# Second mixture of a two-layer MetaFormer kernel: expert weights gathered by GpSimd's indirect DMAs instead of loaded by SyncE's DMAs with a register offset

## The chip, the cores and the metric

The program runs on one core of one Trainium2 chip. The metric is the device time of one execution in microseconds. The median of the kernel before is 3442.44 us over 2 runs (3441.41 and 3443.48).

## The reference

Sixteen images of 64 channels and 56 x 56 pixels pass through two layers. Each layer has a convolution block and a mixture-of-experts block, with norms over the channels ahead of each. Only the second mixture is touched. Its routing is one choice per image: two experts of eight, with two weights.

```python
# x: 16 images, each 3136 tokens of 64 channels; E = 8 experts, hidden size 128
logits = mean(x, axis=1) @ Wr + br
routing_weights = softmax(logits)                    # per image
expected_loads = routing_weights.sum(axis=0) * (N / B)
scale = where(expected_loads > capacity, capacity / expected_loads, 1.0)
routing_weights = softmax(routing_weights * scale)
top_w, top_i = top_k(routing_weights, 2); top_w = softmax(top_w)
h = gelu(x @ W1[e] + b1[e])                          # exact gelu, per expert
y = h @ W2[e] + b2[e]
out = layer_norm(sum over the 2 chosen of top_w * y + x, gamma, beta)
```

## The kernel before

The kernel is written engine by engine, with semaphores by hand, in seven blocks that follow each other with a barrier between them. The image data `X` stays in SBUF for the whole program as 56 tiles of 128 partitions x 448 pixels: 8 pairs of images (the 64 channels of one image on partitions 0 to 63, those of its partner on 64 to 127), 7 tiles to a pair. Blocks 1 to 5 do the first layer and the second convolution. Block 6 (from line 1072) computes the routing on 8 partitions. It also splits the first weight matrices of all 8 experts into a coarse and a fine half and writes them to the DRAM scratch `W1D` as [8 experts, 128 rows, 2, 128]. At its end it writes the chosen expert numbers (`IDX`, 8 pairs x 4) and their weights (`WSEL`) to DRAM.

Block 7 (from line 1202) is the one that changes. It works pair by pair, p = 0 to 7, and each pair uses 4 experts q (two for each image). Two buffers b = p % 2 hold a pair's expert data:

- `w1s`, in the trace `w1sel`: 128 x 256 floats for each q.
- `w2r`, in the trace `w2raw`: 128 x 64 floats for each q.
- `b1s`, in the trace `b1sel`: one float per partition for each q.
- `b2r`, in the trace `b2raw`: two columns, each half of the partitions from another expert.

All loads of one buffer count on one semaphore, `w_in[b]`.

- **SyncE (SP)** issues every DMA of the block: first the expert numbers, the routing weights, gamma and beta, then the tokens of pair 0 (`S[:, k]`, in the trace `tokens<-scr_split`, and `u[:, k]`, `tokens_plus_y<-scr_xn`). `load_weights(p, b)` loads the expert data: for each q a `value_load` of the expert number into registers, then four DMAs whose DRAM address is that register. In the loop, `load_weights(p + 1, 1 - b)` stands at the head of pair p, ahead of the token loads and the stores of that pair.
- **TensorE (PE)** waits for `w_in[b]` at the head of a pair. Then for each tile k it computes `up` (L1318, L1319: hidden layer of expert q, coarse and fine half, into two PSUM buffers) and, one tile behind, `down` (L1332). Behind the 7 tiles come the norm's matmuls `centre` (L154) and `pe_var` (L183).
- **ScalarE (ACT)** applies gelu (L1372) to each hidden tile. After the 7 tiles it squares (L162) and takes reciprocal square roots (L194, L200).
- **VectorE (DVE)** starts by waiting for all seven constant loads (`consts`, 7 x 16). Per tile it adds the tokens (L1411) and finishes a tile of the pair before (L1403). After the 7 tiles it runs `weigh(p + 1, 1 - b)`, which waits for the next pair's `w_in` and scales `w2r` into `w2s` (L1390 to L1395). Then come the norm's three steps for each of the 7 tiles (L205, L208, L215).
- **GpSimd (POOL)** has no instruction in block 7.

The order on each engine is the order of the code: nothing is scheduled by a planner.

## Time and profile before

| | |
|---|---|
| median of 2 runs | 3442.44 us (3441.41 to 3443.48) |
| span of the profiled execution | 3438.1 us; a time of its own is not listed, so what lies around the span is the 3.3 to 5.4 us by which the two runs exceed it |
| TensorE busy | 2756.5 us (80% of the span) |
| ScalarE busy | 1594.6 us (46%) |
| VectorE busy | 1484.2 us (43%) |
| GpSimd busy | 491.1 us (14%), none of it in block 7 |
| block 7 | from 3044.5 us to the end at 3438.1 us: 393.6 us |
| first matmul of block 7 | 3065.8 us |

Times in the rows are microseconds from the start of the span. A busy share over the whole span mixes seven blocks with different limits, so block 7 has to be read by itself: its first 21 us, and one pair after another from there. "SPq" is SyncE's instruction queue. A DMA is shown there with the time of its issue; its landing is given separately.

### The profile page before, as it was taken

To read this page: it belongs to the slowest core of one execution; us is meant where nothing else is said; L and a number is where in the kernel's file an instruction comes from. 1 tells how busy PE (TensorE), PEld (TensorE's weight loads), DVE (VectorE), ACT (ScalarE), POOL (GpSimd) and SP (SyncE) were. 2 spreads that over 40 slices of the span, in tenths; PEclk is the share of its full clock that TensorE was granted. 3 is DMA by queue.
4 is the path that set the end of the run, shared out by engine and by line. 5 is a ranking of instruction groups with operands and counts; after the bars stand their busy time and mean duration, and the time that the engine had idled before them with its cause. 6 is when DMAs were issued, how large, how long until landed. Compare 5 with 4: busy or idle time off the path is not lost. (4 is left out here: it accounts for less than half of the span.)

```text
span 3438.1 us, 42133 instructions
## 1 busy us (share of the span) xinstructions
PE 2756.5 (80%) x12188; PEld 1552.0 (45%) x12188; DVE 1484.2 (43%) x2823; ACT 1594.6 (46%) x2305; POOL 491.1 (14%) x408
## 2 busy tenths in 40 slices
PE   8966334340999999999999999999777777538887
PEld 5622222220555555555555555555555555313333
DVE  6625223331344444444444444443455555414555
ACT  5612222220555555555555555555444444226666
POOL 3303223220000000000000000000254444300000
PEclk9987555655999999999999999999898889769999
DMA  4474222221433333333333333333011111144553
GB/s 143 122 159 105 70 78 69 69 69 60 99 81 81 81 88 87 86 85 86 82 81 81 81 81 81 81 81 81 18 72 72 72 72 72 72 131 142 155 158 103
DMA packets 164007, 308.41 MB, mean 90 GB/s; under 512 B 45698, under 2 KB 156130, under 8 KB 156642
## 3 DMA queue, kind: packets, MB, share of 16 engines
q1 hardware_dynamic: 163938, 307.58, 33.4%
q8 instruction: 32, 0.52, 0.1%
q14 instruction: 37, 0.30, 0.0%
HBM read 210.12 MB, written 97.39 MB: 89 GB/s over the span
## 5 line engine op out<-in xcount | busy, mean ns | idle before, releaser
L776 ACT ACTIVATE hidden<-hidden_psum,b 128x896 f32<-128x896 f32 x896 | 854.4, 1004 | 705.7 <-PE hidden_psum L725 705.6
L739 PE MATMUL y_psum<-hidden,w 128*64 128x448 f32 x3584 | 773.4, 553 | 1.8 <-DVE weighted L842 1.8
L724 PE MATMUL hidden_psum<-tokens,w1hi 128*128 128x448 f32 x1792 | 705.9, 394 | 72.6 <-DMA ident<-in_ident 69.8
L842 DVE SCALAR_TENSOR_TENSOR weighted<-y_psum,b,w_bc 128x448 f32<-128x448 f32 x448 | 306.3, 684 | 923.4 <-PE y_psum L739 909.8
L725 PE MATMUL hidden_psum<-tokens,w1lo 128*128 128x448 f32 x1792 | 660.4, 369 | 0.0
L154 PE MATMUL ln_xc<-X,centre 128*128 (+1 forms) x448 | 261.9, 673 | 332.7 <-DVE X L604 294.2
L724 PEld LDWEIGHTS hidden_psum<-tokens,w1hi 128*128 128x128 f32 x1792 | 336.7, 188 | 391.5 <-ACT hidden L776 294.2
L739 PEld LDWEIGHTS y_psum<-hidden,w 128*64 128x64 f32 x3584 | 217.7, 136 | 350.0 <-issue 244.0
L194 ACT ACTIVATE ln_r<-ln_var,eps 128x448 f32<-128x448 f32 x280 | 177.4, 634 | 405.9 <-PE ln_var L179 287.5
L725 PEld LDWEIGHTS hidden_psum<-tokens,w1lo 128*128 128x128 f32 x1792 | 338.0, 189 | 24.3
L205 DVE SCALAR_TENSOR_TENSOR ln_q<-ln_var,ln_rr 128x448 f32<-128x448 f32 x280 | 173.5, 620 | 318.9 <-DMA scr_split<-lo 211.2
L850 DVE TENSOR_TENSOR X<-X,weighted 128x448 f32 (+1 forms) x448 | 278.1, 621 | 2.9
L154 PEld LDWEIGHTS ln_xc<-X,centre 128*128 128x128 f32 x448 | 91.3, 224 | 398.8 <-issue 367.5
L208 DVE SCALAR_TENSOR_TENSOR ln_g<-ln_q,ln_r 128x448 f32<-128x448 f32 x280 | 233.9, 835 | 9.6
L1038 POOL MEMSET pad_lo<- 128x116 f32 (+1 forms) x4 | 0.8, 268 | 1622.9 <-POOLq L661 1622.9
L934 PE MATMUL conv_psum<-pad_hi,conv_sign 128*128 128x448 f32 x504 | 224.3, 445 | 2.4 <-POOL pad_lo L1046 2.4
L162 ACT ACTIVATE ln_sq<-ln_xc 128x448 f32<-128x448 f32 x224 | 120.4, 537 | 210.3 <-PE ln_xc L154 210.2
L934 PE MATMUL conv_psum<-pad_lo,conv_sign 128*128 128x448 f32 x504 | 204.8, 406 | 0.0
L183 PE MATMUL ln_var<-ln_sq,average 128*128 128x448 f32 x336 | 181.3, 629 | 22.8 <-DVE ln_q L205 17.2
L604 DVE TENSOR_TENSOR X<-X,shifted 128x448 f32 (+1 forms) x56 | 49.2, 883 | 279.6 <-POOL shifted L534 279.6
L200 ACT ACTIVATE ln_rr<-ln_r 128x448 f32<-128x448 f32 x280 | 161.5, 577 | 8.9
L1372 ACT ACTIVATE hidden<-hidden_psum,b1sel 128x448 f32<-128x448 f32 x224 | 130.5, 632 | 75.5 <-PE hidden_psum L1319 75.2
(128 smaller groups left out, 2665.5 us busy)
## 6 DMA issues: line engine op xcount, KB each, us to landing
w_bc<-scr_wtok SPq DMA_DIRECT2D x112, 896.0 KB, 10.9
tokens<-scr_split SPq DMA_DIRECT2D x112, 448.0 KB, 3.7
scr_split<-hi SPq DMA_DIRECT2D x112, 224.0 KB
scr_split<-lo SPq DMA_DIRECT2D x112, 224.0 KB
scr_xn<-xn SPq DMA_DIRECT2D x56, 224.0 KB
tokens_plus_y<-scr_xn SPq DMA_DIRECT2D x56, 224.0 KB, 2.6
out<-out_tile SPq DMA_DIRECT2D x56, 224.0 KB, 2.0
X<-in_x SPq DMA_DIRECT2D x6, 1792.0 KB, 7.6
```

The source lines that it names most:

```text
L154: pe.matmul(self.xc[:, b, 0:TW], CEN[:], x, start=True, stop=True).then_inc(self.centred, 1)
L183: pe.matmul(self.var[:, self.at(m, self.nv), 0:TW], AVG[:], self.sq[:, self.at(m, self.depth)], start=True, stop=True).then_inc(self.var_r ...
L194: act.activation(self.r[:, b], self.var[:, self.at(m, self.nv), 0:TW], ACT.Abs_reciprocal_sqrt, bias=EPS[:, eps_col:eps_col + 1]).then_inc ...
L205: dve.scalar_tensor_tensor(out=self.q[:, b], in0=self.var[:, self.at(m, self.nv), 0:TW], scalar=eps, in1=self.rr[:, b], op0=ALU.add, op1=A ...
L208: dve.scalar_tensor_tensor(out=self.g[:, b], in0=self.q[:, b], scalar=-3.0, in1=self.r[:, b], op0=ALU.add, op1=ALU.mult).then_inc(self.g_d ...
L724: pe.matmul(o, w1hi[:, s * P:(s + 1) * P], S[:, b, a, :], start=True, stop=False)
L725: mm = pe.matmul(o, w1lo[:, s * P:(s + 1) * P], S[:, b, a, :], start=False, stop=True)
L739: mm = pe.matmul(yp[C * a:C * a + C, e % 2, 0:TW], w2[:, e, c, :], hs[:, s % (2 * CH0), a, :], start=(c == 0), stop=(c == CH0 - 1))
L776: act.activation(hs[:, k % (2 * CH0)], hp[:, k % 2, :, 0:TW], ACT.Gelu, bias=b1[:, e, c:c + 1])\
L842: dve.scalar_tensor_tensor(out=pr[:, e % 2], in0=yp[:, e % 2, 0:TW], scalar=b2[:, e:e + 1], in1=WB[:, b, e, :], op0=ALU.add, op1=ALU.mult) ...
L850: dve.tensor_tensor(x, x, pr[:, e % 2], ALU.add).then_inc(summed, 1)
L934: mm = pe.matmul(o, cw[:, t9, :], src[:, pair, ROWS * k + dy:ROWS * k + dy + ROWS, dx:dx + WW], start=(t9 == 0 and part == 0), stop=(t9 == ...
```

## The change

GpSimd takes over the loading of the experts' data in block 7. Instead of one DMA with a register offset it issues indirect DMAs: each of the 128 partitions gets the DRAM row whose number stands in a column of the SBUF tile `rows_now`.

- SP loads the 32 expert numbers into all 128 partitions (`picked`) instead of one, and issues no weight DMA any more. The `value_load`s are gone.
- GpSimd fills `lane` with the partition number. VectorE computes from it and from `picked` the row numbers for all pairs (`expert_rows`: expert x 128 + partition for the first four columns, expert x 64 + partition within the half for the last two). These are eight small instructions, placed behind the wait for the constants.
- GpSimd's `load_weights` copies the pair's six columns to `rows_now`, waits for that copy, and issues 14 indirect DMAs: 12 for the four experts' `w1s`, `w2r`, `b1s`, and 2 of 128 rows for the two columns of `b2r`. Before there were 16 DMAs, four of them for `b2r`, on 64 partitions each. `WIN` follows (14 x 16).
- GpSimd issues the loads of pair 0 and of pair 1 in one go. From then on those of pair p + 1 wait for the last gelu of pair p - 1 (and for `w2_done`, `b2_done`), as SP's did, but with no other DMA ahead of them in the queue.

```diff
-            idr = sbuf(ctx, "idx", [1, NP * 4], I32)
+            picked = sbuf(ctx, "picked", [P, NP * 4], I32)
...
-            WIN = 16 * (4 * 3 + 4)
+            WIN = 16 * (4 * 3 + 2)
...
-                    sp.dma_start(idr[:], IDX.rearrange("(o j) s -> o (j s)", o=1)).then_inc(idx_in, 16)
+                    sp.dma_start(picked[:], IDX.rearrange("j s -> (j s)").partition_broadcast(P)).then_inc(idx_in, 16)
...
-                    def load_weights(p, b):
-                        for q in range(4):
-                            e = sp.value_load(idr[0:1, bass.ds(p * 4 + q, 1)], min_val=0, max_val=E - 1)
-                            sp.dma_start(w1s[:, b, q].bitcast(F32), W1D[bass.ds(e, 1)].rearrange("o p s f -> (o p) s f"))\
-                                .then_inc(w_in[b], 16)
-                            sp.dma_start(w2r[:, b, q], A["w2_l1"][bass.ds(e, 1)].rearrange("o f c -> (o f) c"))\
-                                .then_inc(w_in[b], 16)
-                            sp.dma_start(b1s[:, b, q:q + 1], A["b1_l1"][bass.ds(e, 1)].rearrange("o f u -> (o f) u"))\
-                                .then_inc(w_in[b], 16)
-                            a, s = divmod(q, 2)
-                            sp.dma_start(b2r[C * a:C * a + C, b, s:s + 1],
-                                         A["b2_l1"][bass.ds(e, 1)].rearrange("o c u -> (o c) u")).then_inc(w_in[b], 16)
...
-                            wait(sp, w2_done, p)
-                            wait(sp, b2_done, p)
-                            load_weights(p + 1, 1 - b)
...
                     load_split(0, 0)
-                    sp.wait_ge(idx_in, 16)
-                    load_weights(0, 0)
                     load_tokens(0, 0)
...
+                @block.gpsimd
+                def _(pool):
+                    pool.iota(lane[:], [[0, 1]], base=0, channel_multiplier=1).then_inc(laned, 1)
+                    pool.memset(passed[:], 0.0)
+                    pool.wait_ge(rows_done, 1)
+
+                    def load_weights(p, b):
+                        def gather(dst, src, row):
+                            pool.indirect_dma_start(out=dst, out_offset=None, in_=src,
+                                                    in_offset=bass.IndirectOffsetOnAxis(ap=now[:, b, row:row + 1], axis=0))\
+                                .then_inc(w_in[b], 16)
+
+                        pool.tensor_copy(now[:, b, :], rows_of[:, bass.ds(p, 1), :].rearrange("p o s -> p (o s)"))\
+                            .then_inc(rows_now, 1)
+                        pool.wait_ge(rows_now, p + 1)
+                        pool.tensor_tensor(passed[:], passed[:], passed[:], ALU.add).then_inc(rows_seen, 1)
+                        for q in range(4):
+                            gather(w1s[:, b, q].bitcast(F32).rearrange("p s f -> p (s f)"),
+                                   W1D.rearrange("e p s f -> (e p) (s f)"), q)
+                            gather(w2r[:, b, q], A["w2_l1"].rearrange("e f c -> (e f) c"), q)
+                            gather(b1s[:, b, q:q + 1], A["b1_l1"].rearrange("e f u -> (e f) u"), q)
+                        for t in range(2):
+                            gather(b2r[:, b, t:t + 1], A["b2_l1"].rearrange("e c u -> (e c) u"), 4 + t)
+
+                    def pair(p, b, last):
+                        if not last:
+                            if not isinstance(p, int) or p > 0:
+                                wait(pool, gelu_done, 4 * KT * p)
+                                wait(pool, w2_done, p)
+                                wait(pool, b2_done, p)
+                            load_weights(p + 1, 1 - b)
+
+                    load_weights(0, 0)
+                    every_pair(pool, pair)
...
+                    dve.wait_ge(laned, 1)
+                    dve.wait_ge(idx_in, 16)
+                    dve.tensor_copy(lanef[:, 0:1], lane[:]).then_inc(row_made, 1)
+                    dve.tensor_copy(pickedf[:], picked[:]).then_inc(row_made, 1)
+                    dve.wait_ge(row_made, 2)
+                    chosen = pickedf[:].rearrange("p (j s) -> p j s", s=4)
+                    dve.tensor_scalar(rowf[:, :, 0:4], chosen, float(F1), lanef[:, 0:1], ALU.mult, ALU.add)\
+                        .then_inc(row_made, 1)
+                    for a in range(2):
+                        half = slice(C * a, C * a + C)
+                        dve.tensor_scalar(lanef[half, 1:2], lanef[half, 0:1], float(-C * a), None, ALU.add)\
+                            .then_inc(row_made, 1)
+                        dve.wait_ge(row_made, 4 + 2 * a)
+                        dve.tensor_scalar(rowf[half, :, 4:6], chosen[half, :, 2 * a:2 * a + 2], float(C),
+                                          lanef[half, 1:2], ALU.mult, ALU.add).then_inc(row_made, 1)
+                    dve.wait_ge(row_made, 7)
+                    dve.tensor_copy(rows_of[:], rowf[:]).then_inc(rows_done, 1)
                     dve.tensor_scalar(hgam[:], gam[:], -0.5, None, ALU.mult).then_inc(scaled, 1)
```

SP's queue at the head of block 7, before: behind the constants comes one token load, then the expert numbers one by one, each with its four DMAs. The group of four DMAs stands there four times in all.

```order
L1253 DMA beta<-in_beta 64x1
L1269 DMA tokens4<-scr_split4 128x2x448
L1257 TENSOR_LOAD idx [waits p7_idx]
L1257 ISA x2
L1258 ISA
L1258 DMA w1sel<-scr_w1split 128x256
L1260 ISA
L1260 DMA w2raw<-in_w2_l1 128x64
L1262 ISA
L1262 DMA b1sel<-in_b1_l1 128x1
L1265 ISA
L1265 DMA b2raw<-in_b2_l1 64x1
```

The same place on SP with the change: the token loads of pair 0 follow the constants at once, and the next wait is one for `up` of pair 0.

```order
L1262 DMA beta<-in_beta 64x1
L1265 DMA tokens4<-scr_split4 128x2x448
L1269 DMA tokens_plus_y<-scr_xn4 128x448
L1265 DMA tokens4<-scr_split4 128x2x448
L1269 DMA tokens_plus_y<-scr_xn4 128x448
```

The weight loads have left this queue; 14 token loads stand in a row here.

VectorE at the head of block 7, before: one small instruction behind the wait for the constants, then `weigh(0, 0)`, which waits for the weights.

```order
L1423 TENSOR_SCALAR minus_half_gamma<-gamma 128x1 [waits p7_consts]
L1390 TENSOR_SCALAR w2sel<-w2raw,w_all 128x64 [waits p7_w0,p7_scaled]
L1390 TENSOR_SCALAR w2sel<-w2raw,w_all 128x64 x3
L1392 TENSOR_SCALAR b2tmp<-b2raw,w_half 128x1
L1395 SCALAR_TENSOR_TENSOR b2sel<-b2raw,w_half,b2tmp 128x1 [waits p7_b2a]
```

The same place on VectorE with the change: eight instructions that make the row numbers.

```order
L1451 CAST lane_f<-lane 128x1 [waits p7_idx,p7_laned,p7_consts]
L1452 CAST picked_f<-picked 128x32
L1455 TENSOR_SCALAR expert_rows_f<-picked_f,lane_f 128x8x4 [waits p7_row_made]
L1459 TENSOR_SCALAR lane_f<-lane_f 64x1
L1462 TENSOR_SCALAR expert_rows_f<-picked_f,lane_f 64x8x2 [waits p7_row_made]
L1459 TENSOR_SCALAR lane_f<-lane_f 64x1
L1462 TENSOR_SCALAR expert_rows_f<-picked_f,lane_f 64x8x2 [waits p7_row_made]
L1465 CAST expert_rows<-expert_rows_f 128x48 [waits p7_row_made]
L1466 TENSOR_SCALAR minus_half_gamma<-gamma 128x1
L1416 TENSOR_SCALAR w2sel<-w2raw,w_all 128x64 [waits p7_w0,p7_scaled]
```

All eight stand behind the wait for the constants, and GpSimd's gathers wait for the last of them.

GpSimd's queue in block 7 with the change (before it was empty): the two instructions ahead, the copy that waits for VectorE, and the first gathers.

```order
L1306 IOTA lane 128x1
L1307 MEMSET passed 1x1
L1316 COPY rows_now<-expert_rows 128x6 [waits p7_rows_done]
L1319 TENSOR_TENSOR passed<-passed 1x1 [waits p7_rows_now]
L1312 DMA w1sel<-scr_w1split,rows_now 128x256
L1312 DMA w2raw<-in_w2_l1,rows_now 128x64
L1312 DMA b1sel<-in_b1_l1,rows_now 128x1
```

These three gathers are repeated for each of the four experts, and two `b2raw` gathers follow: 14 in all. The same 16 rows from the copy on then stand once more for pair 1, without a wait for other engines; for pair 2 the copy waits for `p7_gelu`.

## Rows read from the trace of the kernel before

**Rows 1.** Page: span and busy time of each engine.

```profile
span 3438.1 us, 42133 instructions
...
PE 2756.5 (80%) x12188; PEld 1552.0 (45%) x12188; DVE 1484.2 (43%) x2823; ACT 1594.6 (46%) x2305; POOL 491.1 (14%) x408
```

**Rows 2.** Windows, busy us of each engine, granted clock, DMA share, GB/s.

```profile
core 0: us, PE busy (x) PEld busy (x) DVE busy (x) ACT busy (x) POOL busy (x), PEclk, DMA share, GB/s
...
3044.00:3065.00 21.00, 0.00 (x0) 0.00 (x0) 0.15 (x1) 0.00 (x0) 0.00 (x0) 0.50 0.22 54
3065.00:3070.00 5.00, 2.92 (x7) 2.13 (x8) 1.08 (x6) 2.44 (x3) 0.00 (x0) 0.50 0.95 308
3070.00:3075.00 5.00, 4.93 (x14) 2.19 (x13) 0.00 (x0) 2.54 (x4) 0.00 (x0) 0.55 1.05 390
3075.00:3095.00 20.00, 20.00 (x85) 9.03 (x85) 3.42 (x5) 12.30 (x22) 0.00 (x0) 1.00 0.69 215
```

**Rows 3.** Chain that ended last, 3040 to 3072 us: start, us, what.

```profile
3049.81 0.49 SPq L1257
...
3051.34 3.00 SPq L1260
...
3063.02 0.33 SPq L1262
3063.53 2.19 DMA b2raw<-in_b_l
3065.76 0.74 PE hidden_psum L1318
```

**Rows 4.** Timeline 2990 to 3075 us: start, us, engine, line.

```profile
3048.52 0.60 SPq L1253 DMA_DIRECT2D beta<-in_beta  x1
...
3058.09 0.15 DVE L1423 TENSOR_SCALAR minus_half_gamma<-gamma 128x1 f32<-128x1 f32 x1 [16.03 <-DMA beta<-in_beta]
```

**Rows 5.** Waits, 3075 to 3438 us: in total, times, longest.

```profile
DVE tokens_plus_y L1411 <- PE ln_xc_psum L1332: 167.7, 56, 9.6
ACT hidden L1372 <- PE hidden_psum L1319: 74.0, 105, 2.1
```

**Rows 6.** Timeline of VectorE, 3088 to 3120 us.

```profile
3099.05 0.68 DVE L1411 SCALAR_TENSOR_TENSOR tokens_plus_y<-ln_xc_psum,b2sel,tokens_plus_y 128x448 f32<-128x448 f32 x1 [2.67 <-PE ln_xc_psum L1332]
3099.65 0.73 DVE L1390 TENSOR_SCALAR w2sel<-w2raw,w_all 128x64 f32<-128x64 f32 x4
3100.30 0.20 DVE L1392 TENSOR_SCALAR b2tmp<-b2raw,w_half 128x1 f32<-128x1 f32 x1
3100.54 0.22 DVE L1395 SCALAR_TENSOR_TENSOR b2sel<-b2raw,w_half,b2tmp 128x1 f32<-128x1 f32 x1
```

**Rows 7.** Timeline of ScalarE, 3088 to 3120 us.

```profile
3094.31 1.16 ACT L1372 ACTIVATE hidden<-hidden_psum,b1sel 128x448 f32<-128x448 f32 x2 [0.70 <-PE hidden_psum L1319]
...
3114.47 1.28 ACT L1372 ACT_TABLE_LOAD   x1
```

**Rows 8.** DMA issues, 3040 to 3438 us: KB each, median us to landing.

```profile
tokens<-scr_split SPq DMA_DIRECT2D x56, 448.0 KB, 3.7
tokens_plus_y<-scr_xn SPq DMA_DIRECT2D x56, 224.0 KB, 2.6
...
w1sel<-scr_w1split SPq DMA_DIRECT2D x32, 128.0 KB, 2.0
...
b2raw<-in_b_l SPq DMA_DIRECT2D x32, 0.2 KB, 2.2
```

**Rows 9.** Line 208 alone (VectorE, two SBUF inputs), by window.

```profile
2500.00:2600.00 100.00, 18.18 (x21) 0.88 0.19 71
...
3100.00:3400.00 300.00, 30.61 (x49) 0.98 0.50 148
```

**Rows 10.** GpSimd's groups of instructions, whole span: busy, mean ns.

```profile
L1051 POOL TENSOR_TENSOR lo<-xn,hi 128x448 fp32r<-128x448 f32 x56 | 63.8, 1139 | 253.1 <-DVE hi L1012 253.1
...
L1491 POOL MEMSET const-float32-0.0<- 128x1 f32 x1 | 0.1, 99 | 0.2 <-issue 0.2
```

More of the change, by code:

```diff
@@ L1215, in build @@
             bet = sbuf(ctx, "beta", [P, 1])
-            idr = sbuf(ctx, "idx", [1, NP * 4], I32)
+            picked = sbuf(ctx, "picked", [P, NP * 4], I32)
+            pickedf = sbuf(ctx, "picked_f", [P, NP * 4])
+            lane = sbuf(ctx, "lane", [P, 1], I32)
+            lanef = sbuf(ctx, "lane_f", [P, 2])
+            rowf = sbuf(ctx, "expert_rows_f", [P, NP, 6])
+            rows_of = sbuf(ctx, "expert_rows", [P, NP, 6], I32)
+            now = sbuf(ctx, "rows_now", [P, 2, 6], I32)
+            passed = sbuf(ctx, "passed", [1, 1])
             S = sbuf(ctx, "tokens4", [P, KT, 2, TW], F32R)
@@ L1228, in build @@
                                               "scaled", "out"))
+            laned, row_made, rows_done, rows_now, rows_seen = (
+                sem(ctx, "p7_" + s) for s in ("laned", "row_made", "rows_done", "rows_now", "rows_seen"))
             w_in = [sem(ctx, f"p7_w{b}") for b in range(2)]
```

## Prediction

> **What bounds the kernel now.** I read the page first, then windows over block 7, the chain that ended last, the timeline around the first matmul, the waits, and the DMA issues. TensorE is busy for 80% of the span and GpSimd for 14% [rows 1], but those shares average seven blocks, and only block 7 changes. Two stretches of it count.
>
> The head. From 3044 to 3065 us no compute engine works except for 0.15 us of VectorE, TensorE's clock is granted at 0.50 (1.2 GHz), and DMA is at a share of 0.22 [rows 2]. The chain runs through SP's queue. A register load of an expert number takes 0.49 us, one w2 issue holds the queue for 3.00 us, a common issue takes 0.33 us and the next follows 0.51 us after it (3063.02 to 3063.53). The last of 16 weight DMAs starts at 3063.53 and lands 2.19 us later, and the first matmul starts at 3065.76 [rows 3]. VectorE has been held longer than the queue needs for the first loads: its wait for the constants ends with the landing of beta at 3058.09, 9.6 us after the issue at 3048.52 [rows 4]. Before, that was harmless, since VectorE had nothing to give to anyone until the weights came.
>
> The pairs. From 3075 to 3438 us the waits are those between the compute engines: VectorE for `down` (167.7 us), ScalarE for `up` (74.0 us) [rows 5], and no DMA is among them. The expert data of a pair are wanted first by `weigh` on VectorE, at 3099.65 us for pair 1, just behind the last token add [rows 6], and it did not wait there. So SP's weight loads cost something at the head and nothing later.
>
> **The change part by part.**
>
> *SP.* It loses 16 DMAs and four register loads per pair. In the pairs this yields nothing, since nobody waits for SP's transfers. At the head it yields only that the tokens of pair 0 start earlier: seven times 448 + 224 KB [rows 8], 4.7 MB. At the 308 to 390 GB/s seen from 3065 to 3075 [rows 2] that takes 12 to 15 us. Begun behind the constants at 3057 or so, they are in by about 3072, before the first matmul of my forecast. The expert numbers go to 128 partitions instead of one: 128 packets more ahead of the constants, a few tenths of a microsecond that I leave in the range.
>
> *VectorE, index arithmetic.* Eight small instructions stand behind the wait for the constants, and the gathers wait for the last. The nearest rows are the small ones of `weigh`, 0.20 and 0.22 us at 128 partitions [rows 6]: 8 x 0.21 = 1.7 us, from 3058.09 to 3059.8. All of it is on the path. GpSimd's iota runs beside the 14 us of waiting for the constants and costs nothing unless it takes longer than that.
>
> *GpSimd, before the gathers.* A copy of 128 x 6 and a 1 x 1 addition, each behind a semaphore. A memset of one column took 0.10 us [rows 10]; I take 0.25 us each with the handshake, 0.5 us together, to 3060.3.
>
> *GpSimd, the gathers.* This is the term that decides. Call c the time from one gather to the next; 14 of them stand in a row on one queue. No indirect DMA is in this trace. From below I bound c by what SP's common issue takes from one to the next, 0.51 us [rows 3]; from above by the longest issue, 3.00 us, and the 0.18 us that pass between issues, 3.18 us. Between these I take the row of the same engine that handles 128 partitions of a tile, 1.14 us for 128 x 448 [rows 10], since a gather has to make an address for each of 128 rows; with the 0.18 us it is 1.32 us. Then 14 x 1.32 = 18.5 us.
>
> *Landing.* A b2 load lands 2.2 us after its issue, a token load 3.7 us after [rows 8]. Most of the token transfers are over by then, so I take 2.2 us and keep 3.7 us for the upper end.
>
> The first matmul then starts at 3058.1 + 1.7 + 0.5 + 18.5 + 2.2 = 3081.0 us instead of 3065.8, 15.2 us later. What follows is a chain of compute engines and shifts as a whole. The clock does not change this: it was at 0.50 ahead of the first matmul before as well, 0.55 from 3070 and 1.00 from 3075 [rows 2].
>
> The Trainium skill has a figure for c: SBUF — State Buffer, section "A bandwidth-pool intuition that's wrong (but worth ruling out)", gives some 620 ns for a DMA issued from GpSimd alone, and 3100 ns when a VectorE copy in a two-port mode holds the shared port. By the first, an estimate from that page, the delay would be about 8 us instead of 15.2; by the second, about 40. No run here shows either yet.
>
> *Pair 1.* Its 14 gathers follow at once. They are wanted by `weigh` 33.9 us after the first matmul (3065.76 to 3099.65) [rows 3, 6]. They land 14c + 0.5 = 19.0 us after those of pair 0, so 15 us are left. The cover is gone at c = 33.4 / 14 = 2.39 us.
>
> *Pairs 2 to 7.* The gathers start at the end of gelu of two pairs earlier (3094.31 + 1.16 = 3095.5 for pair 2) [rows 7], and `weigh` wants them one pair after 3099.65. A pair takes at most (3438.1 - 3065.8) / 8 = 46.5 us, so the window is 50.7 us for 18.5 + 0.5 + 2.2 = 21.2 us. That is hidden, at no cost. The queue has nothing else in it. GpSimd alone becomes the bound where 14c + 0.5 passes 46.5 us, at c = 3.3 us.
>
> *VectorE beside GpSimd.* The gathers of pairs 2 to 7 begin exactly where the norm of a pair begins, and that norm is a chain through VectorE (from 3095.5 to the table load of the next pair's gelu at 3114.47) [rows 7]. Line 208 reads both inputs from SBUF. It takes 30.61 / 49 = 0.625 us in block 7, where GpSimd is idle, and 18.18 / 21 = 0.866 us where GpSimd works [rows 9]. If each of the 7 such instructions in 6 norms were stretched by these 0.24 us, 10.1 us would be lost; at the other end it is nothing. A gather reads one column of SBUF and not a whole tile, so I take a fifth, 2 us.
>
> The Trainium skill says the same as a rule that speaks against the change: in SBUF — State Buffer, section "Who interferes with whom", a VectorE instruction with two SBUF inputs contends with a GpSimd instruction that reads SBUF, and whichever came first keeps the port for its whole instruction. Rows 9 agree in kind. By that rule the full 10 us are at stake, and they are rival B.
>
> **Sum.** 15.2 + 2 = 17.2 us on 3442.4 gives 3459.6 us. The same on the profiled span is 3438.1 + 17.2 = 3455.3 us; the two runs lie 3.3 to 5.4 us above that span, and I leave that distance as it is.
>
> **The rivals.**
>
> *A: GpSimd is the bound.* It decides from c = 2.39 us. For it speaks that one SP issue did take 3.00 us [rows 3]; against it, that this was one issue behind a queue full of constants, while the common one takes 0.33. At the upper bound, c = 3.18: first matmul at 3058.1 + 2.2 + 44.5 + 3.7 = 3108.5, 42.7 us late, and pair 1's data come 45.0 us after it against 33.9, 11.1 us more: 53.8 us, 3496 us. At c = 4: 56.0 us of gathers, 52.7 us late at the head (landing 2.2), 22.6 at pair 1, and 10 us in each of 6 more pairs, since 56.5 is above 46.5: some 135 us, 3578 us, slower by 4%.
>
> *B: the port.* The head as forecast, and the norms stretched by all of 10.1 us: 15.2 + 10.1 = 25.3, 3468 us. For it: rows 9 and the place of the gathers. Against it: what stretched line 208 there were GpSimd's passes over whole tiles.
>
> *C: faster than before.* The old head was SP's chain, 3049.81 to 3063.53, with the 3.00 us stall and four register loads [rows 3]. The new one begins at 3058.1 and is shorter if the gathers are handed off quickly: it wins where 1.7 + 0.5 + 14c + 2.2 is under 3065.76 - 3058.09 = 7.67 us, so c under 0.23 us. At c = 0.1 it gives 1.9 us, 3440.5 us. Against it: SP's plain DMAs, with one address and no list of rows, take 0.51 us each. At that price, c = 0.51, the delay is 3058.1 + 4.4 + 7.1 - 3065.8 = 3.8 us, 3446 us.
>
> **How the numbers follow.** Forecast (c between 0.51 and 2.39, port cost small): 0.74, at 3460 us. A: 0.12, a third of it beyond 2%. B: 0.07. C and what lies between it and +3.8 us: 0.07, of which less than half is faster than before. 2% of this kernel, about what a measurement can tell from no change, is 68.8 us: slower by that much needs c above about 3.4 us, 0.04. Faster by it has no mechanism, since the whole head from 3044.5 to 3065.8 is only 21 us: 0.01. Within: 0.95. The range starts at 3446 us (c = 0.51) and ends at 3484 us: c = 2.39 gives 3058.1 + 4.4 + 33.5 - 3065.8 = 30.2, with all of the port's 10.1 us some 40, which is 3483. It leaves out most of A and most of C, between 1 and 2 in 10.
>
> **What would show it.** In the profile of the changed kernel: VectorE's first instruction of block 7 at about 3058 us and the eighth done by about 3060; 14 indirect DMAs of GpSimd at 1.3 us each, and the first matmul at about 3081 with the wait put down to the last gather; pair 1's `weigh` without a wait; line 208 at 0.63 us in the norms; the stretch from the first matmul to the end still 372 us. It is wrong if c is far from 1.3 us, if the constants land at another time than 3058 (the gathers hang on it now), if the first gather waits for something on GpSimd that no row here shows, such as the loading of its code, or if the pairs become longer.

## The result, and the profile after

| | before | changed kernel |
|---|---|---|
| median (2 runs each) | 3442.44 us | 3499.63 us (3499.38 to 3499.88) |
| ratio | 1 | 1.0169, 95% interval 1.0149 to 1.0188 |
| profiled execution, span | 3438.1 us | 3499.88 us, span 3498.0 us |

The time is 57.2 us longer, where the sum had 17.2, and it lies outside the range of 3446 to 3484 us. The same program, unedited, was timed again on four chips (the chip of the first timing is not recorded): 3453.55, 3453.32 and 3452.66 us on chips 11, 3 and 12, and 3501.28 us on chip 10. "Before" took 3439.8 to 3440.9 us beside them. So there are two findings: a cost of 11.8 to 13.5 us that came with the change on chips 11, 3 and 12, and 46 to 48 us more that came in two of the five timings. Chip 10 was used at one time only, so whether those belong to the chip or to the time at which it was used is not separated.

The page of the changed kernel, against [rows 1]: GpSimd is busier, there is a queue of 4096 packets for the gathers, and the chain that ended last has a share for something that the profile can't name.

```profile
span 3498.0 us, 41794 instructions
PE 2766.9 (79%) x12188; PEld 1560.2 (45%) x12188; DVE 1489.4 (43%) x2831; ACT 1594.8 (46%) x2305; POOL 604.0 (17%) x538
...
q0 software_dynamic: 4096, 5.27, 0.6%
...
PE 8%; issue 1%; ACT 1%; DVE 1%; another core or an unknown queue 1%; DMA 0%; POOL 0%; SPq 0%; DVEq 0%; ACTq 0%
```

The head, from the chain that ended last (start, us, what). It answers to [rows 3]; behind the constants the register loads and SP's weight DMAs are gone from it, and GpSimd's gathers stand there.

```profile
3049.87 10.22 DMA beta<-in_beta
3060.12 0.15 DVE lane_f L1451
...
3061.44 0.20 DVE expert_rows L1465
3061.64 0.06 issue
3061.69 0.20 POOL rows_now L1316
...
3062.32 1.15 POOL w1sel L1312
3063.47 0.31 issue
3063.77 0.94 POOL w2raw L1312
3064.72 0.30 issue
3065.02 0.95 POOL b1sel L1312
...
3078.74 2.68 DMA b2raw<-in_b_l,rows_now
3081.43 0.04 issue
3081.47 0.74 PE hidden_psum L1344
```

The reader is to see a sum of issue times: a gather is busy for 0.94 us and the next starts 1.25 us after it did, the fourteenth starts at 3078.74 and lands 2.68 us later, and the first matmul is at 3081.47.

Windows over the same stretch and the one behind it, with the columns of [rows 2]:

```profile
3060.00:3070.00 10.00, 0.00 (x0) 0.00 (x0) 1.40 (x9) 0.00 (x0) 6.23 (x8) 0.50 1.06 381
3070.00:3081.00 11.00, 0.00 (x0) 0.00 (x0) 0.00 (x0) 0.00 (x0) 8.62 (x11) 0.50 0.32 106
3081.00:3090.00 9.00, 7.14 (x19) 4.06 (x20) 1.15 (x6) 4.97 (x7) 6.87 (x8) 0.59 0.34 99
3090.00:3096.00 6.00, 1.41 (x6) 0.32 (x6) 0.00 (x0) 0.00 (x0) 4.48 (x6) 0.93 0.14 38
3096.00:3102.00 6.00, 0.15 (x1) 0.18 (x2) 0.05 (x1) 0.85 (x2) 1.24 (x2) 0.50 0.01 0
3102.00:3110.00 8.00, 8.00 (x28) 3.67 (x28) 1.31 (x2) 4.13 (x8) 0.00 (x0) 0.79 0.40 115
```

Between 3090 and 3101 us, inside pair 0's up part, TensorE, VectorE and ScalarE all stand still while GpSimd goes on through pair 1's gathers, and in the end not even a transfer is under way (DMA share 0.01). The timeline of that stretch (start, us, engine, line, operation, and what ended the idle time before):

```profile
3089.14 0.63 ACT L1398 ACTIVATE hidden<-hidden_psum,b1sel 128x448 f32<-128x448 f32 x1 [0.80 <-PE hidden_psum L1345]
...
3090.14 0.36 PE L1345 MATMUL hidden_psum<-tokens,w1sel 128*128 128x448 f32 x1
...
3090.43 0.97 PE L1358 MATMUL ln_xc_psum<-hidden,w2sel 128*64 128x448 f32 x4
...
3096.60 0.94 POOL L1312 DMA_INDIRECT b2raw<-in_b_l,rows_now  x1 [0.30 <-issue]
3101.07 1.34 ACT L1398 ACTIVATE hidden<-hidden_psum,b1sel 128x448 f32<-128x448 f32 x2 [11.29 <-remote]
3101.77 0.38 SPq L1265 DMA_DIRECT2D tokens<-scr_split  x1
3101.82 0.29 PEld L1344 LDWEIGHTS hidden_psum<-tokens,w1sel 128*128 128x128 f32 x1 [11.19 <-issue]
3101.85 0.71 PE L1344 MATMUL hidden_psum<-tokens,w1sel 128*128 128x448 f32 x1 [10.44 <-ACT hidden L1398]
3101.95 0.68 DVE L1437 SCALAR_TENSOR_TENSOR tokens_plus_y<-ln_xc_psum,b2sel,tokens_plus_y 128x448 f32<-128x448 f32 x1 [19.24 <-remote]
```

By the records, whose matmul ends are modelled, TensorE had the up product ready at 3090.5. ScalarE, VectorE and SyncE, which all wait for TensorE here, go on together at 3101, 3.5 us after GpSimd's last gather ended (3096.60 + 0.94). TensorE in turn waited for ScalarE. What comes late is TensorE's hand-over, that is the semaphore signal by which it tells the other engines that a product is ready, and the profile names its releaser "remote". This text calls such a wait a stall.

ScalarE loads its table anew at each change between GELU (line 1398) and the norm (line 194), so these loads cut block 7 into parts. The up part of a pair runs from the first kind to the second, its norm part from there to the next pair. Of the changed kernel, ScalarE's timeline:

```profile
3082.67 1.28 ACT L1398 ACT_TABLE_LOAD   x1 [40.15 <-PE hidden_psum L1345]
3124.92 1.28 ACT L194 ACT_TABLE_LOAD   x1
3143.63 1.28 ACT L1398 ACT_TABLE_LOAD   x1
3173.89 1.28 ACT L194 ACT_TABLE_LOAD   x1
...
3343.18 1.28 ACT L1398 ACT_TABLE_LOAD   x1
```

Lengths of the parts worked out from such rows, in us ("again" is the same program on chip 11 and on chip 10):

| | up, pairs 0 to 7 | norm, pairs 0 to 6 |
|---|---|---|
| before | 30.9 28.9 30.4 30.0 28.8 28.8 28.9 28.9 | 16.6 15.7 15.6 15.6 15.6 15.6 15.7 |
| changed | 42.3 30.3 29.8 30.5 30.8 31.1 30.4 31.4 | 18.7 18.0 20.3 20.0 20.0 21.3 15.7 |
| again, 11 | 30.3 28.9 28.9 30.3 29.9 28.9 28.9 28.9 | 15.7 15.7 15.6 15.6 15.6 15.6 15.7 |
| again, 10 | 43.7 31.1 30.2 30.9 31.0 31.1 30.3 28.9 | 18.7 17.9 19.9 20.0 20.0 22.1 15.7 |

The span grew by 59.9 us: 15.7 at the head, 11.3 in the up part of pair 0, 23.4 in the norm parts of pairs 0 to 5, and 9.4 in the other up parts. The norm parts that grew are those in which GpSimd gathers; pair 6's, with no burst, has its old 15.7.

The 9.4 us are a matter of the clock. Windows over the first 7.5 us of an up part: pair 4 and pair 7 of the changed kernel, then pair 4 before the change (columns of [rows 2]):

```profile
3292.38:3299.88 7.50, 5.52 (x13) 2.66 (x14) 1.93 (x3) 4.98 (x7) 0.00 (x0) 0.50 0.21 61
3441.59:3449.09 7.50, 5.45 (x13) 2.66 (x13) 2.65 (x5) 4.97 (x7) 0.00 (x0) 0.61 0.00 0
...
3250.64:3258.14 7.50, 5.32 (x21) 2.42 (x22) 2.70 (x6) 5.92 (x9) 0.00 (x0) 1.00 0.19 44
```

The granted clock is 0.50 and 0.61 where it was 1.00, and the parts take 30.8 and 31.4 us instead of 28.8 and 28.9. Six of the seven up parts behind pair 0 follow a lengthened norm part; pair 7's does not. The kernel before has such a spell too, without any gather, in pairs 2 and 3 (30.4 and 30.0 us).

### The profile page after: what moved, and what is told of

It reads as the page before. It is cut to its first block and busy times, and to the rows that moved or that the text cites. A ratio compares the mean times of both kernels' runs of the same rounds, so it can differ in the third digit from the quotient of the medians.

```text
span 3498.0 us, 41794 instructions
## 1 busy us (share of the span) xinstructions
PE 2766.9 (79%) x12188; PEld 1560.2 (45%) x12188; DVE 1489.4 (43%) x2831; ACT 1594.8 (46%) x2305; POOL 604.0 (17%) x538
## 3 DMA queue, kind: packets, MB, share of 16 engines
q0 software_dynamic: 4096, 5.27, 0.6%
## 5 line engine op out<-in xcount | busy, mean ns | idle before, releaser
L1344 PE MATMUL hidden_psum<-tokens,w1sel 128*128 128x448 f32 x224 | 104.4, 466 | 93.3 <-DMA b2raw<-in_b_l,rows_now 47.4
```

The costliest lines, as they stand in the source:

```text
L1344: pe.matmul(hp[:, q % 2, 0:TW], w1s[:, b, q, 0, :], S[:, k, q // 2, :], start=True, stop=False)
```

## The experiments

The labels e11, e12, e17 and e18 gave no result; e13, e14, e19 and e20 are the same kernels.

**e1, only the gathers.** The kernel before, with 14 unused gathers on GpSimd in the place of each burst:

```
+ def pair(p, b, last):
+     if not last and not (isinstance(p, int) and p == 0):
+         wait(pool, gelu_done, 4 * KT * p)
+         ...
+         for size in [256, 64, 1, 256, 64, 1, 256, 64, 1, 256, 64, 1, 256, 64]:
+             pool.indirect_dma_start(out=spare[:, at:at + size], ...)
```

> The kernel before, with SP loading the expert data as it did, and in addition 14 indirect DMAs of 128 rows (rows 0 to 127, into a tile that nobody reads) on GpSimd at the end of gelu of pairs 0 to 5, where the changed kernel has its gathers. In the changed kernel the norms of pairs 0 to 5 (from the load of the reciprocal-root table to the next load of the gelu table) grew from 15.6 to 18.0 to 21.3 us, and what TensorE had finished was seen late by the others. Theory A, the gathers themselves hold up TensorE's completions, whatever is gathered: the norms of pairs 0 to 5 grow by 2 to 6 us here too, the head stays (first matmul at 3065.8), 3465 to 3475 us in all. Theory B, the changed order of SP's DMAs or the dependence on late data does it: norms stay at 15.6, 3442 us. Theory C, GpSimd shares a port with VectorE: the norms grow, but line 208 shows it, with a mean above 0.70 us instead of 0.625.

Measured on chip 11: 3441.18 us, ratio 0.9998 (0.9986 to 1.0009), norm parts 15.6 to 16.6. A gather as such takes nothing from TensorE on that chip.

**e2, gathers spread.** Two behind the first GELU of each tile instead of 14 in a row.

```
+ if pace and n % 2 == 0:
+     wait(pool, gelu_done, 4 * (KT * (p - 1) + n // 2) + 1)
```

> The changed kernel, with the gathers of pair p + 1 spread over the up phase of pair p: two for each of its seven tiles, instead of 14 in a row at the end of gelu of pair p - 1. Pair 0 has its 14 in a row as before, but the second 14 no longer follow at once. Theory A with a backlog (only a long row of gathers holds up TensorE): the stall of 11.3 us in pair 0 and those of the norms go, and what is left is the head: 3442 + 16 = 3458 us. Theory A without a backlog (each gather costs its share): the same stall moves into the up phases, and the total stays at 3490 to 3500 us. Theory B (late data): nothing changes against the changed kernel or it becomes worse, 3500 us or more, since the data come later now.

Measured: 3452.92 us, 1.0034 (1.0021 to 1.0048), no long part. I took it then for a cure; e5 shows that there was nothing to cure on that chip.

**e3, index arithmetic early.** VectorE's eight instructions stand ahead of its wait for the constants.

```
+ dve.wait_ge(laned, 1)
+ ... (the eight instructions)
  dve.wait_ge(consts, 7 * 16)
```

> The changed kernel, with the eight VectorE instructions that make the row numbers put ahead of the wait for the constants, so that they wait for the expert numbers alone. My account of the head: the gathers hang on the landing of beta at 3060.1; the expert numbers should be there by about 3049, so the gathers start some 10 to 11 us earlier and the first matmul comes at about 3071 instead of 3081.5. The rest of the loss (11 us in pair 0, 23 in six norms, 9 in the later up phases) stays: 3488 to 3490 us. Rival: 28 gathers in a row then run beside the loading of 4.7 MB of tokens and of the tiny constants, and take longer, so that less than 6 us are won: 3494 us or more.

Measured: 3447.43 us, 1.0021 (1.0010 to 1.0032). The first table load came at 3072.11 instead of 3082.67, so the head gave what it should (the first gather started 13.3 us earlier, at 3048.98, but the last one took 5.46 us to land instead of 2.68, beside DMA at a share of 1.06); but the long parts, which I had expected to stay, were gone with all bursts in place. That 41 us miss raised the question whether they belong to the program.

**e4, plain DMAs on GpSimd.** The loads of the burst with fixed expert numbers 0 to 3; the choice of experts is left out.

```
- gather(w2r[:, b, q], A["w2_l1"].rearrange("e f c -> (e f) c"), q)
+ pool.dma_start(w2r[:, b, q], A["w2_l1"][q:q + 1].rearrange("o f c -> (o f) c")).then_inc(w_in[b], 16)
```

> The changed kernel, with plain DMAs issued by GpSimd in place of the indirect ones: same number, same destinations, same sizes, same waits. The experts are fixed (0 to 3), so the choice of experts is left out. If the stall of TensorE belongs to every DMA that GpSimd issues: norms of 18 to 21 us and about 3490 to 3500 us, as in the changed kernel. If it belongs to the indirect form alone (a list of 128 rows): norms of 15.6 us, no stall in pair 0, and with an issue time of 0.5 to 1.25 us for each DMA a first matmul between 3070 and 3081: 3447 to 3458 us.

Measured: 3447.34 us, 1.0023 (1.0011 to 1.0034), issues of 0.54 us that follow each other without a gap, no long part. With indices GpSimd is busy for 0.94 us instead of 0.54 with a DMA, and the next starts after 1.25 us.

**e5, the changed kernel again**, with **e6** (early index arithmetic, but gathers held until the constants are in) and **e7** (pair 1's burst held until pair 0's second GELU tile).

```
  pool.wait_ge(rows_done, 1)
+ pool.wait_ge(scaled, 1)        # e6
...
+ if isinstance(p, int) and p == 0:        # e7
+     pool.wait_ge(gelu_done, 8)
```

> The changed kernel itself, nothing edited. Beside it, on this chip, three kernels with the same gathers in the pairs ran at 3447 to 3453 us with pairs as long as before, while the changed kernel had taken 3499.6 us. Theory A (the stalls belong to the program: some order in time or place that only the changed kernel has): 3499 us again, norm parts of pairs 0 to 5 at 18 to 21 us, the up part of pair 0 at 42 us. Theory B (the stalls belong to the chip or the session in which the changed kernel was timed): 3457 to 3459 us here, which is 3442.4 plus the 15.7 us of the later first matmul, and no stall in the pairs.

> The kernel with the index arithmetic ahead of the constants, but GpSimd waits for VectorE's first operation behind the constants before it starts gathering. The gathers run at the times of the changed kernel, from about 3061 on, and only the place of the index arithmetic in VectorE's program differs. Theory A1 (the time at which the gathers run against the token loads and the other engines decides): the stalls return, 3497 to 3500 us. Theory A2 (the order of VectorE's instructions, or the wait of GpSimd on the index arithmetic behind the constants, decides): no stalls, first matmul at about 3080.5, 3457 to 3459 us.

> The changed kernel with one edit: pair 1's 14 gathers wait for the second tile of pair 0's GELU, so that 28 gathers in a row become 14 and 14. Theory A3 (the long first burst starts a state that each later burst renews): no stall anywhere, 3457 to 3460 us. Theory A4 (each burst of 14 makes its own stall in the norm part): pair 0's first stall of 11 us goes or moves behind the second burst, the norm parts of pairs 1 to 5 stay at 18 to 21 us, 3485 to 3500 us.

Measured, all on chip 11: 3453.55 us (1.0039, 1.0025 to 1.0052), 3453.80 us (1.0039) and 3457.47 us (1.0047, 1.0029 to 1.0065), no stall in any. Theory B of e5 holds: the program alone does not make the long parts. (Of the three kernels that its expectation calls ones with the same gathers, only e2 and e3 are; e4 has plain DMAs.) e5 was even 3.5 us below its expectation. Its first matmul, in TensorE's timeline:

```profile
3080.42 0.74 PE L1344 MATMUL hidden_psum<-tokens,w1sel 128*128 128x448 f32 x1 [47.45 <-DMA b2raw<-in_b_l,rows_now]
```

Its span is 3451.3 us, so from there to the end are 370.9 us, 372.3 before. e6 and e7 say nothing on the stalls, since nothing stalled there without them either.

**e8, e9, e10 (chip 3): the changed kernel once more, and the head by other means.** In e9 SyncE loads pair 0's weights as before the change and only pairs 1 to 7 are gathered; in e10 pair 0's are shared.

```
+ for q in range(4):        # SyncE, pair 0; e10 leaves w1 and b2 to GpSimd, with the early arithmetic
+     e = sp.value_load(idr[0:1, bass.ds(q, 1)], min_val=0, max_val=E - 1)
+     sp.dma_start(w2r[:, 0, q], A["w2_l1"][bass.ds(e, 1)]...).then_inc(w0x, 16)
```

> The changed kernel once more, nothing edited, to see how often the long pairs come. Theory A (a condition outside the program, which held when the changed kernel was first timed and not later): either 3453 us with norm parts of 15.6 us, or 3499 us with norm parts of 18 to 21 us, nothing between, and the other kernels that run beside it share the fate of their gathers. Theory B (chance from one execution to the next): times that scatter between 3453 and 3500 us over the rounds.

> Pair 0's weights are loaded by SyncE with loaded expert numbers, as before the change; pairs 1 to 7 are gathered by GpSimd as in the changed kernel. Theory A (the head is the whole loss where there are no stalls): first matmul within 1 us of that before the change, and 3440 to 3442 us, the same as before. Theory B (the bursts in the pairs cost something too, which the earlier runs hide in their scatter): 3444 us or more. If the stalls come, the norm parts of pairs 0 to 5 are long here too, and the time is about 3480 us.

> The index arithmetic ahead of the constants, and pair 0's weights shared between two engines: GpSimd gathers w1 and b2 (6 gathers, 7.5 us at 1.25 us each), SyncE loads w2 and b1 with a loaded expert number (8 loads instead of 16). Pairs 1 to 7 are gathered. Theory A (the head is a sum of issue times, so two engines share it): first gather at about 3052, first matmul at 3061 to 3063 instead of 3065.8, 3436 to 3439 us, a little faster than before. Theory B (SyncE's program is the bound again, by its value loads and the time its DMAs take to issue behind the 0.45 MB token load): first matmul at 3065 to 3067, 3440 to 3443 us.

Measured: 3453.32 us (1.0041, 1.0026 to 1.0056); 3439.80 us (1.0001, 0.9992 to 1.0010); 3438.43 us (0.9998, 0.9989 to 1.0007). e9 settles what the change costs on an undisturbed chip: all of it is pair 0's head, and the 98 gathers for pairs 1 to 7 cost nothing that these runs can tell. e10's time lies in the range of theory A, but its first matmul at 3065.15 is theory B's, and its ratio is no gain: A, a head shared to advantage, did not occur. GpSimd's first gather was at 3050.68, earlier than hoped, but SyncE's part became the bound. One of its loads held the queue for 2.98 us, the last was issued at 3061.59, and it landed 3.52 us later:

```profile
3060.35 0.27 SPq L1299
3060.65 0.15 SPq L1299
...
3061.59 3.52 DMA b1sel<-in_b_l
3065.10 0.04 issue
3065.15 0.74 PE hidden_psum L1356
```

No version beats the kernel before by more than these runs can tell.

**e13 and e14 (chip 12): a fourth time, and the suspected cost doubled.** e14 is e1 with 28 gathers of one number each.

```
- for size in [256, 64, 1, 256, 64, 1, 256, 64, 1, 256, 64, 1, 256, 64]:
+ for size in [1] * 28:
```

> The changed kernel again, nothing edited. It has run at 3453.6 and 3453.3 us on two chips without a long pair, and at 3499.6 us when it was first timed. Theory A (the long pairs belong to a condition that is rare): 3453 us and norm parts of 15.6 us. Theory B (they belong to a chip, so that a third chip has a chance to show them): 3499 us and norm parts of 18 to 21 us.

> The kernel before the change, with 28 gathers of one number per partition that nobody reads, on GpSimd behind the last GELU of each of pairs 0 to 5. That is 35 us of gathers in a row in each pair, twice the burst of the changed kernel, over the norm part and half of the next up part. Theory A (gathers take nothing from TensorE as long as nothing else is wrong): 3440 to 3442 us, norm parts of 15.6 to 16.6 us. Theory B (a burst draws on something that 14 gathers just don't exhaust, the room for their descriptors say, and the first timing of the changed kernel lay beyond that point): norm parts or up parts longer by 2 us or more, 3455 us or more.

Measured: 3452.66 us (1.0037, 1.0023 to 1.0051) and 3441.28 us (1.0004, 0.9994 to 1.0014). On this chip 35 us of gathers in a row are still free.

**e15 and e16 (chip 10): the stalls come back.** e16 moves each burst beside an up part (the wait is for the pair's second GELU, where the text below says the third).

```
- if not isinstance(p, int) or p > 0:
-     wait(pool, gelu_done, 4 * KT * p)
+ wait(pool, gelu_done, 4 * KT * p + 2)
```

> The changed kernel again, nothing edited. Theory A (the long pairs belong to a rare condition): 3453 us and norm parts of 15.6 us. Theory B (they belong to a chip that the runs have not met again so far): 3499 us and norm parts of 18 to 21 us, if this is that chip.

> The changed kernel with the 14 gathers of pair p+1 behind the third GELU of pair p, beside the up part, where TensorE is busiest, instead of behind the last GELU of pair p-1. Theory A (no condition holds that makes gathers cost TensorE something): the same as the changed kernel beside it, 3452 to 3455 us. Theory B (gathers in a burst hold TensorE's results back wherever it is dense): up parts of pairs 0 to 6 of 31 to 42 us in place of 28.9, norm parts of 15.6 us.

Measured: 3501.28 us (1.0175, 1.0158 to 1.0192) and 3530.54 us (1.0261, 1.0244 to 1.0278), beside "before" at 3440.62. e15 is the first timing over again, down to the parts in the table. In e16 the long parts moved with the bursts: the up parts of pairs 0 to 6 take 37.2 to 42.4 us, all norm parts 15.6 to 15.7, and pair 7's up part, without a burst, 28.9. ScalarE's timeline for pairs 2 and 3:

```profile
3190.09 1.28 ACT L1397 ACT_TABLE_LOAD   x1
3232.42 1.28 ACT L194 ACT_TABLE_LOAD   x1
3248.05 1.28 ACT L1397 ACT_TABLE_LOAD   x1
3290.40 1.28 ACT L194 ACT_TABLE_LOAD   x1
```

Up parts of 42.3 us, 13.4 more than 28.9, and a norm part of 15.63 between them, as before the change. Inside such a part, windows of pair 2, with a burst from 3193.54 to 3210.80:

```profile
3196.00:3202.00 6.00, 6.00 (x28) 2.61 (x24) 1.28 (x2) 2.55 (x5) 4.69 (x5) 1.00 0.37 127
3202.00:3208.00 6.00, 2.26 (x8) 0.80 (x4) 0.00 (x0) 1.27 (x2) 4.47 (x6) 0.86 0.42 131
3208.00:3214.00 6.00, 1.76 (x4) 0.33 (x4) 1.35 (x2) 0.64 (x2) 2.19 (x3) 0.50 0.17 48
3214.00:3220.00 6.00, 5.95 (x14) 2.92 (x16) 1.28 (x2) 2.99 (x5) 0.00 (x0) 0.51 0.20 72
3220.00:3232.00 12.00, 12.00 (x50) 5.23 (x48) 3.83 (x6) 6.54 (x13) 0.00 (x0) 1.00 0.56 171
```

TensorE runs on for the first 9 us of the burst, falls to 2.26 and 1.76 us of 6 in its second half, comes back 2.6 us after the burst (3213.36) and then works at the lower clock level for some 6 us more (granted 0.51), which is 1.2 GHz. The chain that ended last shows the same three steps there:

```profile
3202.47 2.40 issue
...
3206.25 3.59 issue
3209.88 3.50 another core or an unknown queue
3213.38 0.62 ACT hidden L1397
```

They are 9.5 of the 13.4 us; the slower matmuls behind them are the rest.

**e19 and e20 (chip 14): e1 and e4 repeated, in the hope of such a chip.**

> The kernel before with 14 unused gathers on GpSimd behind the last GELU of each of pairs 0 to 5; on a chip without the trouble it took 3441.2 us. On the chip of the long pairs: Theory A (the gathers alone hold TensorE's results back): norm parts of pairs 0 to 5 of 18 to 21 us, 3465 to 3485 us. Theory B (it takes the changed kernel's other parts too, its waits or the loads that others wait for): 3441 us.

> GpSimd issues the weights as plain DMAs with fixed expert numbers (the choice of experts is left out); on a chip without the trouble it took 3447.3 us. On the chip of the long pairs: Theory A (what hurts is that GpSimd writes descriptors, for any DMA of its own): norm parts longer by some 40% of what the gathers add, since the issue takes 0.54 instead of 1.25 us each, 3460 to 3475 us. Theory B (what hurts is the gather by indices): norm parts of 15.6 us, 3447 us.

Measured: 3442.21 us (1.0000, 0.9991 to 1.0010) and 3446.34 us (1.0018, 1.0008 to 1.0027), norm parts of 15.6 to 16.5. Neither kernel has run beside a kernel that stalls, so this tells nothing of the cause.

**e21 and e22 (chip 5): both cases in one kernel.** e21 paces the gathers for the even pairs and leaves those for the odd ones in a burst; e22 has SyncE load the even pairs beside unused gathers.

```
+ load_weights(p + 1, 1 - b, pace=b == 1)        # e21
...
+ if b == 0: load_weights(p + 1, 1)        # e22: GpSimd, odd pairs
+ else:      idle(p + 1)                   # 14 unused gathers; SyncE loads the pair
```

> The changed kernel, in which the gathers for the even pairs 2, 4 and 6 are paced, two behind the first GELU of each tile of the up parts of pairs 1, 3 and 5; those for the odd pairs stay in a burst. On a chip without the trouble: 3452 to 3454 us, all parts as before the change. On the chip of the long pairs: the up part of pair 0 at 42 us and the norm parts of pairs 1, 3, 5 at 18 to 21 us show it; Theory A (only a dense row of gathers holds TensorE's results back, since they must be consumed before the next is through): up parts of pairs 1, 3, 5 at 29 to 31 us, about 3478 us. Theory B (each gather costs TensorE about a microsecond wherever it is): those up parts at 39 to 42 us, about 3515 us.

> The changed kernel, in which the even pairs' weights are loaded by SyncE with loaded expert numbers as before the change (pair 0's too), and GpSimd does 14 unused gathers behind the last GELU of pairs 0, 2 and 4; the odd pairs' weights are gathered. On a chip without the trouble: 3440 to 3442 us. On the chip of the long pairs: norm parts of pairs 1, 3, 5 at 18 to 21 us show it; Theory A (the gathers alone do it, whoever reads them): norm parts of pairs 0, 2, 4 at 18 to 21 us too. Theory B (it takes the engines' waits on gathered data, or the weights not loaded by SyncE): 15.6 us there.

Measured: 3455.46 us (1.0040, 1.0026 to 1.0054) and 3442.76 us (1.0003, 0.9994 to 1.0013), 1.5 and 0.8 us above what was expected without the trouble. Even the changed kernel's own bursts in them did not stall, so chip 5 was without it. Whether pacing cures it, and whether unused gathers cause it, were not decided.

## Why the prediction was right in part, and where it failed

**The head was right in kind, and nearer in number than its terms.** The constants landed at 3060.1 instead of 3058.1. The arithmetic took 1.5 us (1.7 forecast), copy and addition with their hand-overs 0.7 us (0.5), the landing 2.7 us (2.2). From the first gather to the start of the fourteenth went 16.4 us, where the sum had 18.5. Of this difference 0.8 us is c (1.26 us on average, 1.32 forecast) and 1.3 us a miscount: a landing is counted from the start of the last issue, so 13 steps stand ahead of it and not 14. Constants 2.0 us late and gathers 2.1 us short cancelled, and the first matmul came at 3081.47 (3081.0 forecast). That is luck. Moreover 1.35 of the 2.0 us are chance and not the change: SyncE came to the issue of beta at 3049.87 instead of 3048.52, and in the five profiles of this program that issue lies between 3047.35 and 3050.65. Counted from it, the first matmul came after 31.6 to 31.9 us in all five, 17.2 us before the change: 14.4 to 14.6 us more, where 15.2 were forecast. The token loads, which I had begin at 3057, were issued from 3050.51 on.

The choice of c by the GpSimd row of [rows 10] rather than by SyncE's 0.51 us carried this. That the row, an arithmetic pass over 128 x 448, takes nearly as long as a gather is not more than a coincidence by what these runs show. e4 shows why SyncE's row would have misled: GpSimd's plain DMA takes 0.54 us, its indirect one 0.94, with 0.30 more to the next. The Trainium skill's figure for a DMA issued from GpSimd alone (SBUF — State Buffer, section "A bandwidth-pool intuition that's wrong (but worth ruling out)"), some 620 ns, is near the 0.54 us of e4, and half of the 1.25 us from one gather to the next. (The two delays that the prediction works out from that page, 8 and 40 us, are made with and without the 0.18 us between issues; with it in both they are 7.9 and 42.7 us.)

**Pair 1 and pairs 2 to 7 were covered.** `weigh` waited for no gather behind pair 0, and e9 puts the cost of the gathers in the pairs between -2.8 and +3.4 us. Rival A did not occur.

**The port cost nothing.** Line 208 took 0.625 us in all 56 instances of the changed kernel, as where GpSimd is idle in [rows 9]. The 2 us that I had added for it were wrong, and so was rival B. That GpSimd reads a column of indices while VectorE has two inputs in SBUF did not show; the rule of the Trainium skill that the prediction cites (SBUF — State Buffer, section "Who interferes with whom") shows here only where GpSimd works on whole tiles, 0.866 us in [rows 9].

**The step that failed** is "What follows is a chain of compute engines and shifts as a whole", with "That is hidden, at no cost" for pairs 2 to 7. From the first matmul to the end it took 416.5 us instead of the forecast 372. On chips 11, 3 and 12 the step holds: 369.7 to 371.2 us, and a time of 3452.7 to 3453.6 us, near the forecast 3460 and inside the range. On chip 10, and where the changed kernel was first timed, TensorE's hand-overs stop late in each burst. Shown is that the stall does not come with the program alone (the same program, with "before" unchanged beside it), that on chip 10 it repeats from run to run (3499.69 to 3503.96 us), and that it follows the bursts there when they are moved. That it is the chip, and not the time at which chip 10 was used, is not shown. Of the four terms of the 59.9 us, the head's 15.7 were in my sum; 11.3 in pair 0, beside whose up part pair 1's burst runs, 23.4 in six norm parts, and 9.4 elsewhere were not. The last is TensorE at the lower clock level at the start of up parts (granted 0.50 in the window of pair 4), mostly behind a lengthened norm part; pair 7's 2.5 us follow none, and are of the kind that the kernel before has in pairs 2 and 3. I had named longer pairs as a risk, and gave it neither a mechanism nor a price. That the time stayed within 2% of before (0.95) came true all the same, at 1.7%.

**What stays open** is the mechanism. The first matmul on chip 10 came at 3082.36 and each gather took as long as on chip 11, so GpSimd is not slower there. Line 208 took 0.624 to 0.626 us on chip 10 too, so VectorE's port did not cost anything there either. The index arithmetic and its place are not excluded as a part of the cause, since e3 and e6 ran only where nothing stalled. Unused gathers, plain GpSimd DMAs and paced gathers have not met a chip that stalls, so it isn't shown that indices, or a dense row of them, are needed for it. Nor is it shown that the stall comes without the records of the profiler: every timed execution of the changed kernel has its span and clock from them.

## What to carry to other kernels

Cost a gather that GpSimd issues by its own rows, 1.25 us from one to the next at 128 rows, and count those that stand ahead of the first use, with the landing from the start of the last one; where later ones have a whole stage to hide in, leave the first stage's loads with the queue that had them (e9 costs nothing, the changed kernel 12 to 14 us). A time from one chip at one time is no more than that: where a trace shows waits whose releaser it can't name, run the same program on others before explaining them by the edit. A burst of indirect DMAs beside TensorE is a risk that became real in two of five timings here, at 46 to 48 us (77 us in e16).

## What the runs showed of the hardware

- An indirect DMA of 128 rows keeps GpSimd busy for 0.94 us whether a row has 1 or 64 numbers (a median of 0.99 us for 256), and the next starts 1.25 us after it did; a plain one takes 0.54 us, and the next follows without a gap (e4).
- On chip 10 a burst of 14 of them lengthens an up part by 8 to 13.4 us (e16) and a norm part by 2 to 6 us (e15). TensorE's hand-overs stop not at its start but some 9 us into it (e16, and pair 0 of the first timing), and in e16's pairs 2 to 5 they are back 2.6 us after its end. On chips 11, 3 and 12 the same bursts do nothing (up parts 28.8 to 30.5 us, norm parts 15.6 to 15.7).
- The place of the bursts counts there: beside the up parts (e16) the kernel takes 29 us more than with them in the norm parts (e15).
- After such a stall the granted clock is 0.5 (1.2 GHz) for some 6 us (0.51 from 3214 to 3220 in e16), which adds to it.
